# A windowed-attention block on one core: normalisation and projection of a row one row later, key stores split by the term they read

## The reference

```
y  = x + attention(layernorm over channels(x))
out = y + spectral_mixer(layernorm over channels(y))
```

## Time and profile before

| | us |
|---|---|
| median of 3 runs (range) | 4819.89 (4807.23 to 4825.66) |
| profiled execution | 4811.22 |
| its span | 4809.4 |
| mean granted clock of PE in it | 0.876 |

### The profile page before, as it was taken

One profiled execution on the slowest core, in us unless ns is written; L12 is line 12 of the kernel. 1 busy time (PEld: TensorE's weight loads), 2 busy tenths in 40 slices (PEclk: granted clock), 3 DMA queues, 4 the chain that ended last, 5 costly groups with the idle time before them and its releaser, 6 DMA issues. The chain is left out here.

```text
span 4809.4 us, 162661 instructions
## 1 busy us (share of the span) xinstructions
PE 3586.2 (75%) x52286; PEld 2589.5 (54%) x52286; DVE 2391.0 (50%) x3981; ACT 2266.9 (47%) x5101; POOL 1265.3 (26%) x4160
## 2 busy tenths in 40 slices
PE   4337688677777777877887788778893798998965
PEld 1125455455555555554554555455661487887855
DVE  2155475466556545754764575466562533333322
ACT  1025466555555555655555565556781232333310
POOL 1013243234334333433343243234441000000000
PEclk9998898888888888888888898888996799999987
DMA  2314333333443343344334334333326645345469
GB/s 79 106 54 106 101 89 97 97 97 85 102 102 93 89 100 96 87 103 104 91 87 105 95 94 95 97 97 88 61 42 96 224 86 103 79 97 101 79 138 291
DMA packets 800004, 485.09 MB, mean 101 GB/s; under 512 B 550265, under 2 KB 779002, under 8 KB 791962
## 3 DMA queue, kind: packets, MB, share of 16 engines
q1 hardware_dynamic: 739874, 408.07, 36.8%
q10 hardware_dynamic: 59360, 67.44, 4.8%
HBM read 264.58 MB, written 209.19 MB: 99 GB/s over the span
## 5 line engine op out<-in xcount | busy, mean ns | idle before, releaser
L556 POOL COPY Ksel<-Kexp 96x128 int32 x3136 | 927.9, 338 | 1780.2 <-PE ps L1184 1626.7
L919 DVE TENSOR_REDUCE Mx<-ps 128x2 f32<-128x512 f32 x1568 | 1058.0, 686 | 502.0 <-PE ps L1162 495.5
L768 ACT ACTIVATE Pr<-ps 128x1024 f32<-128x1024 f32 x784 | 800.9, 1022 | 977.3 <-PE ps L1184 826.9
L1182 PE MATMUL ps<-Qbd,Ksel 96*128 96x128 bf16 x6272 | 896.6, 232 | 22.3 <-issue 21.0
L1184 PE MATMUL ps<-MT,each 84*128 84x128 bf16 x6272 | 896.9, 232 | 1.2 <-issue 1.0
L689 ACT ACTIVATE Vsel<-Vpx 64x72 f32 x3136 | 815.3, 260 | 135.2 <-DMA Vpx<-v_dram 65.9
L1162 PE MATMUL ps<-Ksel,Qbd 96*128 96x256 bf16 x3136 | 643.9, 289 | 143.1 <-POOL Ksel L556 93.8
L1182 PEld LDWEIGHTS ps<-Qbd,Ksel 96*128 96x128 bf16 x6272 | 658.9, 105 | 109.3 <-issue 100.1
L1184 PEld LDWEIGHTS ps<-MT,each 84*128 84x128 bf16 x6272 | 659.8, 105 | 101.8 <-issue 94.0
L1201 PE MATMUL ps<-Pr,Vsel 128*9 128x64 f32 x25088 | 532.3, 228 | 117.5 <-ACT Vsel L689 64.3
L1201 PEld LDWEIGHTS ps<-Pr,Vsel 128*9 128x9 f32 x25088 | 387.4, 94 | 310.5 <-issue 309.9
(11 more groups left out here) (168 smaller groups left out, 3653.0 us busy)
## 6 DMA issues: line engine op xcount, KB each, us to landing
q_dram<-Pq SPq DMA_DIRECT2D x336, 112.0 KB
k_dram<-Pk SPq DMA_DIRECT2D x336, 112.0 KB
Kexp<-k_dram ACTq DMA_DIRECT2D x112, 336.0 KB, 4.3
Qbd<-q_dram SPq DMA_DIRECT2D x224, 168.0 KB, 4.2
Vpx<-v_dram ACTq DMA_DIRECT2D x112, 252.0 KB
s_dram<-S SPq DMA_DIRECT2D x8, 2048.0 KB, 13.1
Sin<-s_dram SPq DMA_DIRECT2D x64, 256.0 KB, 4.7
z_dram<-Zs SPq DMA_DIRECT2D x128, 128.0 KB, 3.7
```

What stands on the lines that cost most here:

```text
L556: nc.gpsimd.tensor_copy(dst[:, w, :, k, :], src[:, :, bass.ds(win[k] * (PX // 2), PX // 2)])\
L768: nc.scalar.activation(Pr[k][:].rearrange("q c p h x -> q (c p h x)"), ps[:, ST0 + 2 * k:ST0 + 2 * k + 2, :].rearrange("q a b -> q (a b)") ...
L919: nc.vector.tensor_reduce(Mx[u % 2][:, 2 * half:2 * half + 2, w], ps[:, half, :].rearrange("q (p k) -> q p k", p=2), AX.X, ALU.max).then_i ...
L1182: mm(out, Ksel[u % 2][:, w, p, 2 * c:2 * c + 2, :].rearrange("r k x -> r (k x)"), query(u, w, p), start=True, stop=False)
```

## The change

- `project`, `add` and `normalise` of a row are done not in the next row (windows 6, 6 and 5) but in the one after it, at windows 3, 3 and 2. The projection comes right before `mean2`.
- The late norm moves by one row with them: rows 10 to 13, and rows 0 to 2 of the next pair for the last three. At the end of attention one more projection and one more late norm are done behind the last window.
- TAPS_AT moves one tap from window 2 to window 5.
- The one semaphore of the key stores becomes three. `store_k` takes a term: the three stores of term 0 go out right behind `store_q`, those of terms 1 and 2 where all six stood. `first_k` waits for the stores of term 0 alone, `second_k` for those of term 1, `third_k` for term 2; the load of the keys waits for all.

```diff
-TAPS_AT = [2, 2, 2, 1, 1, 1, 0]
+TAPS_AT = [2, 2, 1, 1, 1, 2, 0]
...
-            if u in (0, 1):
-                return None if first else (d - 1, NWIN - 2 + u)
-            if u >= UNITS - 5:
-                return (d, u - (UNITS - 5))
+            if u < 3:
+                return None if first else (d - 1, NWIN - 3 + u)
+            if u >= UNITS - 4:
+                return (d, u - (UNITS - 4))
...
-            def store_k(e, i):
-                hold(sp, "sp", k_part2, e * NWIN + i + 1)
-                for n, (_, part) in enumerate(TERMS):
-                    sp.dma_start(k_dram[at(e), :, n, :, i * ROW:i * ROW + ROW].rearrange("a b c x -> (a b) c x"),
-                                 Pk[:, part, :]).then_inc(k_stored, 16)
+            def store_k(e, i, part):
+
+                ready, done = ((k_part0, k0_stored), (k_part1, k1_stored), (k_part2, k2_stored))[part]
+                hold(sp, "sp", ready, e * NWIN + i + 1)
+                for n, (_, term) in enumerate(TERMS):
+                    if term == part:
+                        sp.dma_start(k_dram[at(e), :, n, :, i * ROW:i * ROW + ROW].rearrange("a b c x -> (a b) c x"),
+                                     Pk[:, part, :]).then_inc(done, 16)
...
                 if behind:
                     store_q(e, u - 1)
+                    store_k(e, u - 1, 0)
...
                 if behind:
-                    store_k(e, u - 1)
+                    store_k(e, u - 1, 1)
+                    store_k(e, u - 1, 2)
...
             def first_k(t):
                 hold(act, "act", k_ready, t + 1)
-                hold(act, "act", k_stored, t * (6 * 16))
+                hold(act, "act", k0_stored, t * (3 * 16))
...
             def second_k(t):
                 hold(act, "act", k_res, t + 1)
+                hold(act, "act", k1_stored, t * (2 * 16))
...
+                    if w == 3 and both:
+                        add(d if u > 1 else d - 1, (u - 2) % UNITS, g - 2)
                     if w == 3 and prev:
                         invert(g - 1)
...
-                    if w == 6 and prev:
-                        add(d if u > 0 else d - 1, (u - 1) % UNITS, g - 1)
...
-                    if w == 5 and prev:
-                        normalise(g - 1, (u - 1) % 2)
+                    if w == 2 and both:
+                        normalise(g - 2, u % 2)
...
+                    if w == 3 and both:
+                        project(g - 2, (u - 2) % UNITS, *empty)
+                        empty = (proj_added, g - 1)
                     if w == 3 and load is not None:
...
-                    if w == 6 and prev:
-                        project(g - 1, (u - 1) % UNITS, *empty)
-                        empty = (proj_added, g)
```

More of the change, by code:

```diff
@@ L219, in attention @@
         q_stored = sem("q_stored")
-        k_stored = sem("k_stored")
+        k0_stored = sem("k0_stored")
+        k1_stored = sem("k1_stored")
+        k2_stored = sem("k2_stored")
         vs_stored = sem("vs_stored")
@@ L274, in attention @@
         MISC_PREP = 7 * NWIN + 2 + NWIN
-        MISC_FIRST = MISC_PREP + UNITS - 1 + 2 * (NWIN - 2)
+        MISC_FIRST = MISC_PREP + UNITS - 2 + 2 * (NWIN - 3)
         MISC_DUO = MISC_PREP + UNITS + 2 * NWIN
@@ L429, in _ @@
                 store_q(0, i)
-                store_k(0, i)
+                for part in range(3):
+                    store_k(0, i, part)
                 store_vs(0, i)
@@ L464, in slot @@
                 if u == 0 and not first:
-                    store_u(d - 1, LAST - 2)
+                    store_u(d - 1, LAST - 3)
                 if before is not None:
@@ L511, in _ @@
             d = duos - 1
-            store_u(d, LAST - 2)
-            store_x2(d, NWIN - 2)
+            store_u(d, NWIN - 4)
+            store_x2(d, NWIN - 3)
             sums_spread(duos * UNITS - 1, 1)
@@ L516, in _ @@
             rsums_spread(duos * UNITS - 1, 1)
+            store_u(d, NWIN - 3)
+            store_x2(d, NWIN - 2)
             store_u(d, NWIN - 2)
@@ L604, in slot @@
                     if w == 3 and u <= LAST and not last:
-                        square(e * NWIN + u, e * NWIN - 9 + min(u, 2))
+                        square(e * NWIN + u, e * NWIN - 10 + min(u, 3))
                     if w == 4 and load is not None:
@@ L613, in _ @@
             bodies(pool, body)
+            square2(tiles - 3, tiles)
             square2(tiles - 2, tiles)
@@ L700, in load_k @@
             def load_k(e, b, i):
-                hold(act, "act", k_stored, (e * NWIN + i + 1) * (6 * 16))
+                hold(act, "act", k0_stored, (e * NWIN + i + 1) * (3 * 16))
+                hold(act, "act", k1_stored, (e * NWIN + i + 1) * (2 * 16))
+                hold(act, "act", k2_stored, (e * NWIN + i + 1) * 16)
                 act.dma_start(Kexp[b][:, :, i * ROW:i * ROW + ROW],
@@ L806, in _ @@
             copy_o(duos * UNITS - 1, 1, 1)
-            for t in (tiles - 2, tiles - 1):
+            for t in (tiles - 3, tiles - 2, tiles - 1):
                 log_var2(t)
@@ L860, in third_k @@
                 hold(dve, "dve", k_part1, t + 1)
+                hold(dve, "dve", k2_stored, t * 16)
                 nc.vector.tensor_tensor(Pk[:, 2, :], Rk[:, :], Pk[:, 1, :], ALU.subtract).then_inc(k_part2, 1)
@@ L991, in slot @@
                 prev = not (first and u == 0)
+                both = not (first and u < 2)
                 fresh = not last and u <= LAST
@@ L1059, in _ @@
             g = duos * UNITS - 1
+            normalise(g - 1, 0)
+            add(duos - 1, UNITS - 2, g - 1)
+            centre2(tiles - 3, NWIN - 3)
+            invert(g)
+            scale2(tiles - 3)
             centre2(tiles - 2, NWIN - 2)
-            invert(g)
             scale2(tiles - 2)
@@ L1248, in slot @@
                     empty = (q_res, lag + 1)
+                elif late(d, u - 1, first) is not None:
+                    done = late(d, u - 1, first)
+                    empty = (std2_ready, done[0] * NWIN + done[1] + 1)
                 else:
-                    empty = (proj_added, g - 1)
+                    empty = (proj_added, g - 2)
                 for w in range(NWIN):
@@ L1318, in _ @@
             weighted(g, UNITS - 1, LAST)
-            mean2(tiles - 2, NWIN - 2, g - 1, proj_added, g)
+            project(g - 1, UNITS - 2, std2_ready, tiles - 3)
+            mean2(tiles - 3, NWIN - 3, g - 2, proj_added, g)
+            variance2(tiles - 3, cen2_ready, tiles - 2)
+            mean2(tiles - 2, NWIN - 2, g - 1, std2_ready, tiles - 2)
             variance2(tiles - 2, cen2_ready, tiles - 1)
```

## The result

The changed kernel is slower: 4901.84 us (median of 4 runs, 4886.65 to 4916.39) against 4816.62 (4807.23 to 4825.66) of the kernel before beside it, a ratio of 1.018 with a 95% interval of 1.016 to 1.020. The forecast was 4705, range 4595 to 4810. The profiled span is 4899.4 us with a mean granted clock of 0.881 (4809.4 and 0.876 before).

A forecast was written before the change was run, and what follows sets the result against it. The prediction took the chain from key stores to Pk to Rk as the bound, with PE busiest at 75%. Gain 267 less costs 147 and 17 made 103 us: 4811 - 103 = 4708, given as 4705, range 4595 to 4810.

The forecast's parts named there:

- What bounds the kernel: Attention rows: Pk waits 249.1 us for the key stores of the row before, and Rk, computed from Pk, 300.6 us.
- the list: Signs of being right: Pk's wait for k_dram gone, Rk's below 80 us, rows 2 to 5 at 26 to 31 us.
- Term a: Key stores at a row's first windows: splitting them removes the wait for Pk, gaining 267 us, bounds 130 and 290.
- Term e: Four busy DMA engines in rows 3 to 6: last key stores, Vt and Qbd arrive later, costing 17 us.
- Rival 1: The four DMA engines decide: waits return for Pk's second term, Vt or Qbd, half of term a goes; 4785 us, chance 0.22.
- Term b: Projection at window 3 instead of 6: 1.4 us new time per row, less what window 6 gives back.
- Terms b and c: Window 3: projection 1.4 us a row; second norm behind it waits for the add, 1.4 more in late-norm rows.
- Term d: Row 2 carries a late norm, costing 4.2 us; row 9 none, giving back some 2; net 2.2.
- The tail: Behind the last weighted product: one more norm in series, 6 us, with the projection 8.
- Rival 3: Window 3 of late-norm rows: PE's stop before mean2 brings half clock, 2.8 us a row; 4856 us, chance 0.09.
- Its sign that would show it: Over the profiled run: a mean clock lower than 0.876 would show rival 3.
- Rivals 2 and 4: 2: window 3 hides its additions, 4600 us, chance 0.13; 4: Pk waits as before, 4958 us, chance 0.03.

## Why the prediction was wrong

By the two halves the sum 267 - 147 - 17 = 103 reads: split +250, move -147. Measured, with the move priced on the kernel before as in the prediction: +141 and -229, together -88, the result. (In the other order it is +60 and -148. That the last number is the forecast's is luck: it holds the cure of a wait for Rb that the prediction did not foresee.) Both halves lie inside the bounds that the prediction gave them (130 to 290, and 60 to 230), both near the bad end. The range was built from one bound falling at a time; its lower gain with its higher cost, 130 - 230 = -100, would have held the time.

- **What bounds the kernel: right.** One chain from the key stores to Pk to Rk. Its wait went as the list said.
- **Term a, wrong in size.** "What is late next there is nothing up to a row of 25.6 us" failed. (The 25.6 also takes the 0.5 us for the clock off twice, for the 8.1 holds it already: 34.2 - 8.1 = 26.1.) Row 3 came out at 27.35, but the others did not follow: rows 2 to 5 gained 27.5 us per pair at window 0 and gave 6.8 back at windows 1 and 2, where waits for Vt (26.1 us over the span), Qbd (66.6, from 39.4) and the later Pk terms (33.2 and 13.9) now stand. Net 20.7 a pair, 145 us in seven, instead of 220. Rows 6 to 8 got 2.9 us per pair at windows 0 to 2, some 20 us of their 47: row 7 wins 6.3 at window 0 and gives 5.9 back at window 1, since VH comes when it comes; the run with VH first shows that queueing was a cause, and that its load had to be moved to gain.
- **Term e, the right mechanism at the wrong size and place.** Four runs show what the order is worth: the same bytes in four orders give 0.988, 0.964, 0.988 and 0.950. (What fewer bytes would give was not run.) I had asked how full the four engines are, and not who stands behind whom. Rival 1 (chance 0.22) has the waits come back and half of term a gone, which is what the changed kernel shows (141 of 267 us), but not that the sums' round trip would be a victim, and its 4785 us fail with the price of the move. In the changed kernel Rb has a row more, so it shows there only in the smaller waits.
- **Term b, the step whose mechanism failed.** The prediction itself says that the projection "fills the time in which PE waits for DVE's copy", and then takes time back for emptying that place: 5 x 1.6 in rows 2 to 6, 3.1 in rows 0 and 1, 3.7 in row 7, 5 x 0.65 in rows 8 and 10 to 13 (row 9's -0.6 leaves its 0.65 out, and the 1.9 of row 1 stands in no row), 18.1 per pair. It got 7.0: 11.1 too little, 78 us in seven pairs. Rows 0 to 6, mostly read from the earlier trace rows, were nearly right: 8.9 of 11.1. Row 7 gave 1.4 of 3.7, and rows 8 to 13 did not give 3.3 but lost 3.3: there the copy comes when DVE has done its taps and maxima, whether PE is busy or not, and PE now stands idle for up to 2.00 us meanwhile. The run that leaves the product out at the old place shows that nothing was to be had there, and the run that shifts it inside window 6 that taking it out of the hole costs 2.9%.
- **Terms b and c at window 3.** Forecast 14 x 1.4 + 7 x 1.4 + 7 x 0.4 = 32.2 per pair, measured 40.2. The stop is as forecast (1.18 us, 66.7 us in 55 against about 1 us x 53). What was missing is, by its size, the clock: at 2.22 us on average instead of 1.69 the projection takes 14 x 0.53 = 7.4 us more per pair, of the 8.0 missing. (The second means behind it got 2.0 us shorter meanwhile, so this is a match in size and not shown by a run of its own.)
- **Term d: not separable.** Row 2 grew by 2.3 us with 5.8 forecast, less what term a gave it; row 9 did not give back 2 but grew by 2.0. The tap that moved from window 2 to 5 was not run apart either.
- **The tail:** 8 us forecast, 1 measured.
- **Rival 3 (0.09)** named the right place and half the price: a stop and a projection at half clock in late-norm rows. But it was priced on top of a full term a, so its time, 4856, is still low. Its sign that would show it, a mean clock under 0.876, did not come (0.881): from the clock record, time at 1.2 GHz went from 41.3 to 19.1 us per pair in rows 2 to 5 and from 31.0 to 52.2 in rows 9 to 13. The mean hid both. The Trainium skill, "TensorE: Matmul & The Clock Gate", section "HAM oscillation — how this bites in real kernels", stood beside it in the prediction. It speaks of a clock that falls again at each of many waits for DMA; row 10 (0.93 to 0.83), with stops of 1.2 and 2.0 us, is consistent with such a fall, but no run here isolates the stops as its cause.
- **Rivals 2 and 4:** no. Window 3 hides nothing, and the change does what it says.

What stays open: how the 40 us of window 3 divide between the lost cover, the stop and the clock. Per pair the runs give 22.1 for the place at window 2 (441.3 to 419.2, with its own new wait inside and 11.5 of it in window 1), 6.4 in window 3 for the stop (87.1 to 80.7), 10.3 there for the product (87.1 to 76.8), and none of these is free of the clock, which changed in every run. How much each hole is worth at constant clock wasn't tried.

## What to carry to other kernels

Before moving work, ask what it covers where it stands: here a projection between a transpose and the reader of its copy cost nothing, and where it stood outside of such a wait its window grew by 2.9 us a row, stops and clock included. Where transfers shared a few DMA engines, as here, splitting a wait changed who is first in line; write down for every store that goes earlier which small, urgent transfer now stands behind it, and put that one in front. And when two terms of a sum have wide bounds, let the range hold both at their bad end together.

## What was not expected of the hardware

- A product of 448 columns left out where it had covered a wait made the kernel 0.5% slower, with a mean granted clock of 0.855 instead of 0.876. At the new place leaving it out also lowered the clock, 0.881 to 0.858.
- 14 KB of sums took 6.5 us to DRAM with three key stores of 112 KB more in front, and 3.2 us without them.
- The wait for the copied maxima, 1.4 us on average and up to 2.2, is put down to POOL's gather by the profile in 195 places; the copy's end, some 0.5 us ahead of the scores, names the true one, and the gather they need had ended over 8 us before.
